# One new order for the last four images, u in two copies, and the up convolution in eight matrices from image 6 on

## The reference, cut to what matters

```
x = x + conv(group_norm(x))        # per image: repeat 2x, 12x12 up filter, leaky relu, 12x12 down filter, every second pixel
t = x as 1024 tokens of 32 channels
t = t + attention(layer_norm(t))   # causal, one head, 1024 x 1024 scores per image
t = t + ffn(layer_norm(t))         # per image: 16 experts each take their 8 best tokens, pool them by the softmax
                                   # over tokens, run two layers (gelu), and add the result back to those tokens
```

## Time and profile before

| | |
|---|---|
| median of 3 runs | 364.86 us (364.76 to 365.97) |
| the profiled execution | 366.71 us, of which the span from first to last instruction is 364.8 us |
| PE busy | 323.3 us (89%), weight loads 249.3 us (68%) |
| DVE, ACT, POOL busy | 258.4 us (71%), 186.6 us (51%), 127.3 us (35%) |
| up convolutions (line 923 into psB) | 480 matmuls |
| granted PE clock, mean | 0.954 |

### The profile page before, as it was taken

One profiled execution on the slowest core, in us unless ns is written; L12 is line 12 of the kernel. 1 busy time (PEld: TensorE's weight loads), 2 busy tenths in 40 slices (PEclk: granted clock), 3 DMA queues, 4 the chain that ended last, 5 costly groups with the idle time before them and its releaser, 6 DMA issues.

```text
span 364.8 us, 8376 instructions
## 1 busy us (share of the span) xinstructions
PE 323.3 (89%) x3357; PEld 249.3 (68%) x3357; DVE 258.4 (71%) x523; ACT 186.6 (51%) x257; POOL 127.3 (35%) x94
## 2 busy tenths in 40 slices
PE   2279998799999999999898998989998686996995
PEld 1168886587778778786767786858685444754894
DVE  2679779957766877859784877566988888265622
ACT  1043355457547574747664647466755647441510
POOL 6134635232444338454311374532116400043000
PEclk9999999999999999999999999999999999896655
DMA  4920000011010010101010101010103100100123
GB/s 123 195 49 3 23 22 16 15 17 31 16 18 23 8 32 2 31 2 34 15 16 2 31 0 32 2 31 5 26 15 74 34 2 6 42 2 29 47 68 88
DMA packets 35906, 11.16 MB, mean 31 GB/s; under 512 B 24431, under 2 KB 35741, under 8 KB 35869
## 3 DMA queue, kind: packets, MB, share of 16 engines
q1 hardware_dynamic: 33152, 9.98, 11.4%
q10 hardware_dynamic: 2717, 0.66, 1.3%
HBM read 5.72 MB, written 4.21 MB: 27 GB/s over the span
## 4 chain that ended last, share of the span: by engine, by line
PE 75%; DVE 10%; DMA 6%; issue 3%; ACT 3%; POOL 1%; SPq 1%; ACTq 1%; DVEq 0%; POOLq 0%
PE psB L923 14%; PE psA L923 13%; PE psB L1056 10%; PE psB L1036 8%; PE psA L1021 7%; PE psA L1114 5%; PE psA L1092 3%; PE psB L1073 2%; DVE negmax L784 2%; PE psA L1063 2%; PE psB L1039 2%; PE psA L911 2%; PE psA L1014 2%; PE psA L1024 2%; PE psB L1001 1%
## 5 line engine op out<-in xcount | busy, mean ns | idle before, releaser
L784 DVE TENSOR_REDUCE negmax<-psA 128x1 f32<-128x512 f32 (+7 forms) x128 | 90.7, 751 | 35.7 <-PE psA L1024 34.9
L596 ACT ACTIVATE Pp<-psB 128x1024 f32<-128x1024 f32 (+1 forms) x80 | 73.6, 938 | 34.9 <-PE psB L1039 30.8
L923 PE MATMUL psB<-xin,UU 128*128 128x224 f16 (+1 forms) x480 | 56.2, 276 | 0.2 <-issue 0.2
L923 PE MATMUL psA<-y,DD 128*128 128x224 f16 (+1 forms) x480 | 55.1, 273 | 0.0
L1021 PE MATMUL psA<-zK,yQ 128*128 128x512 f16 (+1 forms) x192 | 46.9, 326 | 7.1 <-DVE negmax L784 2.2
L923 PEld LDWEIGHTS psB<-xin,UU 128*128 128x128 f16 x480 | 46.9, 99 | 7.9 <-DVE xin L725 0.5
L1036 PE MATMUL psB<-yQ,zK 128*128 128x512 f16 (+1 forms) x192 | 47.2, 330 | 5.1 <-DMA yQ<-rows 2.8
L923 PEld LDWEIGHTS psA<-y,DD 128*128 128x128 f16 x480 | 46.8, 98 | 5.5
L486 POOL TENSOR_TENSOR zrstd<-zrstd,power 128x8 f32<-128x8 f32 x16 | 27.2, 1700 | 53.8 <-DVE zrstd L762 53.8
L566 ACT ACTIVATE y<-psB 128x1024 f16<-128x1024 f32 x16 | 16.4, 1023 | 44.5 <-PE psB L923 44.5
L508 POOL TENSOR_TENSOR y<-y 128x1024 f16<-128x1024 f32 x16 | 34.1, 2132 | 9.6 <-ACT y L569 9.6
(11 more groups left out here) (162 smaller groups left out, 499.4 us busy)
## 6 DMA issues: line engine op xcount, KB each, us to landing
x_all<-in_x_dram SPq DMA_DIRECT2D x4, 512.0 KB, 4.3
normalised_tokens<-z SPq DMA_DIRECT2D x16, 128.0 KB, 1.8
zV<-normalised_tokens SPq DMA_DIRECT2D x64, 32.0 KB, 2.2
out_dram<-x_all SPq DMA_DIRECT2D x8, 256.0 KB, 2.3
yQ<-rows SPq DMA_DIRECT2D x32, 2.0 KB
Pp<-filter_tables ACTq DMA_DIRECT2D x4, 121.9 KB, 4.2
w_halves<-y SPq DMA_DIRECT2D x12, 32.0 KB, 1.8
cst<-shape_constants SPq DMA_DIRECT2D x1, 326.5 KB, 4.3
```

The lines of the kernel that those rows point to most:

```text
L596: nc.scalar.activation(Pp[:, n % 2, UOFF[e[2]]:UOFF[e[2]] + N], slot(e)[:, 0:N], ACT.Exp).then_inc(b_drained, 1)
L784: ins = nc.vector.tensor_reduce(negmax[:, n % 2, m - 1:m], s[:, at:at + P * m], X, ALU.max, negate=True)
L923: ins = nc.tensor.matmul(within(out_cols, -shift), m, within(v, shift), start=i == 0, stop=i == len(matrices) - 1)
```

## The change

From image 6 on (`PLAIN_UP`), blocks t = 1 and 2 take one matrix for both neighbours: the taps of k = -1 for row blocks 2 and 3 are copied by two DMAs into the empty rows of the matrix of k = +1 (`filter_wrap`), and ScalarE makes moved copies of the image for it, partitions 0 to 63 moved one way, 64 to 127 the other (`mixed`, two activations an image, on a tile that POOL has set to zero). That makes 24 matmuls, all but six with 256 columns. Images 0 to 5 keep 30, but the three matmuls of k = +1 at t = 1 and 2 use only partitions 0 to 63, because the other rows of that matrix now hold something else. `wT` of groups 0 to 2 goes from ring B to ring A, its copy from ACT to DVE. u has two copies, by group; att has storage of its own, and the wait for the logits goes from `proj` to `uT`. The steps end at t = 11, and one new list holds everything from the last score of image 13 on. The core of the diff:

```diff
+LAST_STEP = 12
...
+PLAIN_UP = 6
...
+def mixture(ahead):
+
+    return lambda t: ("mixed", t + ahead) if PLAIN_UP <= t + ahead < B else None
...
-        once(-8, "xT", 3), batch(0, "prob", 0), group(6, "logit_max"), batch(2, "yQ"), batch(-1, "pv"),
+        once(-8, "xT", 3), batch(0, "prob", 0), mixture(5), group(6, "logit_max"), batch(2, "yQ"), batch(-1, "pv"),
...
-LAST = [("prob", B - 1, 0), ("pv", B - 2), ("prob", B - 1, 1), ("wT", G - 2), ("prob", B - 1, 2), ("mean", G - 1, 0), ("pool", G - 2),
-        ("prob", B - 1, 3), ("prob", B - 1, 4), ("square", G - 1, 0), ("proj", G - 1, 1), ("mean", G - 1, 1), ("dev", G - 1, 0),
-        ("pv", B - 1), ("hidden", 0), ("square", G - 1, 1), ("proj", G - 1, 2), ("mean", G - 1, 2), ("square", G - 1, 2), ("dev", G - 1, 1),
-        ("scale", G - 1, 0), ("experts", 0), ("dev", G - 1, 2), ("scale", G - 1, 1), ("turned", 0), ("scale", G - 1, 2), ("scatter", 1, 0),
-        ("uT", G - 1), ("logit_max", G - 1), ("logits", G - 1), ("select", G - 1), ("scatter", 1, 1), ("logit_exp", G - 1),
-        ("route", G - 1), ("scatter", 2, 0), ("scatter", 2, 1), ("wT", G - 1), ("pool", G - 1), ("scatter", 0, 0), ("hidden", 1), ("scatter", 0, 1), ("experts", 1),
-        ("turned", 1), ("scatter", G - 1, 0), ("scatter", G - 1, 1)]
+LAST = [("score", 13, 2), ("z_rstd", 15), ("prob", 12, 0), ("yQ", 14), ("dev", 2, 0), ("pv", 11), ("prob", 12, 1), ("score", 13, 0), ("prob", 12, 2),
+        ("proj", 2, 1), ("split_z", 15), ("score", 14, 4), ("shift", 13), ("prob", 12, 3), ("score", 14, 1), ("zK", 15), ("prob", 12, 4), ("score", 14, 3),
+        ("score", 14, 2), ("prob", 13, 0), ("yQ", 15), ("pv", 12), ("prob", 13, 1), ("score", 14, 0), ("mean", 2, 1), ("prob", 13, 2), ("score", 15, 4),
+        ("shift", 14), ("prob", 13, 3), ("score", 15, 1), ("prob", 13, 4), ("score", 15, 3), ("dev", 2, 1),
+        ("score", 15, 2), ("prob", 14, 0), ("pv", 13), ("score", 15, 0), ("prob", 14, 1), ("w1", 0), ("shift", 15), ("prob", 14, 2), ("w1", 1), ("uT", 2),
+        ("prob", 14, 3), ("proj", 3, 0), ("logits", 2), ("prob", 14, 4), ("mean", 3, 0), ("square", 3, 0),
+        ("prob", 15, 0), ("logit_max", 2), ("pv", 14), ("prob", 15, 1), ("proj", 3, 1), ("select", 2), ("logit_exp", 2), ("prob", 15, 2), ("mean", 3, 1),
+        ("route", 2), ("prob", 15, 3), ("dev", 3, 0), ("prob", 15, 4), ("wT", 2), ("square", 3, 1), ("pool", 2),
+        ("pv", 15), ("proj", 3, 2), ("dev", 3, 1), ("mean", 3, 2), ("hidden", 0), ("square", 3, 2),
+        ("scale", 3, 0), ("experts", 0), ("dev", 3, 2), ("scale", 3, 1), ("turned", 0), ("scale", 3, 2), ("scatter", 1, 0),
+        ("uT", 3), ("logit_max", 3), ("logits", 3), ("select", 3), ("scatter", 1, 1), ("logit_exp", 3),
+        ("route", 3), ("scatter", 2, 0), ("scatter", 2, 1), ("wT", 3), ("pool", 3), ("scatter", 0, 0), ("hidden", 1), ("scatter", 0, 1), ("experts", 1),
+        ("turned", 1), ("scatter", 3, 0), ("scatter", 3, 1)]
...
-    for t in range(-9, B - 1):
+    for t in range(-9, LAST_STEP):
...
-    return events + LAST
+    return [e for e in events if e not in LAST] + LAST
...
-ON_A = ("xT", "small", "dnT", "gn_mean", "gn_var", "proj", "score", "uT", "shift", "down", "pool", "yQ",
+ON_A = ("xT", "small", "dnT", "gn_mean", "gn_var", "proj", "score", "uT", "shift", "down", "wT", "pool", "yQ",
         "experts", "turned", "scatter")
-ON_B = ("up", "prob", "logits", "pv", "tok", "zK", "hidden", "wT")
-A = {e: n for n, e in enumerate(e for e in EVENTS if e[0] in ON_A)}
-BU = {e: n for n, e in enumerate(e for e in EVENTS if e[0] in ON_B)}
+ON_B = ("up", "prob", "logits", "pv", "tok", "zK", "hidden")
+LAST_WT = ("wT", G - 1)
+A = {e: n for n, e in enumerate(e for e in EVENTS if e[0] in ON_A and e != LAST_WT)}
+BU = {e: n for n, e in enumerate(e for e in EVENTS if e[0] in ON_B or e == LAST_WT)}
...
+        mixed = sb("mixed", [P, 2, 2, H, JW], F16)
...
-        att = uT
+        att = sb("att", [P, S])
...
-        u = sb("u", [P, KT, P])
+        u = sb("u", [P, 2, KT, P])
...
-        def part_of_u(first, last):
-            return u[:, :, C * first:C * last].rearrange("p k (b c) -> p b k c", b=last - first)
+        def part_of_u(n, first, last):
+            return u[:, n % 2, :, C * first:C * last].rearrange("p k (b c) -> p b k c", b=last - first)
...
+        def filter_wrap(r):
+
+            q, n = slice(C * r, C * r + C), r - 1
+            return (UU[q, :, SPAN - n:SPAN, :, :].rearrange("p i m q t -> p i (m q t)"),
+                    U_parts[q, :, 0:n, :, :].rearrange("p i m q t -> p i (m q t)"))
+
+        def mixture_halves(n):
+
+            at = BC * (n % GB)
+            v = xin[:, n // GB % 2, :].bitcast(F16).rearrange("p (i n) -> p i n", i=2)[:, :, at:at + BC].rearrange("p i (h j) -> p i h j", j=JW)
+            return [(mixed[rows, n % 2, :, :, to:to + JW - 1], v[rows, :, :, 1 - to:JW - to])
+                    for rows, to in ((slice(0, 2 * C), 0), (slice(2 * C, P), 1))]
...
+                    if g == 0:
+                        for r in (R - 2, R - 1):
+                            place_to, place_from = filter_wrap(r)
+                            sp.dma_start(place_to, place_from).then_inc(UU_wrapped, 16)
...
+                if name == "dnT":
+                    nc.gpsimd.memset(mixed[:, :, :, :, :], 0.0).then_inc(mixed_zero, 1)
...
-                    if g >= 1:
-                        pool.wait_ge(a_filled, A["pool", g - 1] + 1)
-                    nc.gpsimd.tensor_tensor(part_of_u(first, last), by_image(t2_all[:, g, :], first, last), per_token(nmean[:, e[2], :], last - first),
+                    if g >= 2:
+                        pool.wait_ge(a_filled, A["pool", g - 2] + 1)
+                    nc.gpsimd.tensor_tensor(part_of_u(g, first, last), by_image(t2_all[:, g, :], first, last), per_token(nmean[:, e[2], :], last - first),
...
+                if name == "mixed":
+                    if n < PLAIN_UP + 2:
+                        act.wait_ge(mixed_zero, 1)
+                    else:
+                        act.wait_ge(b_filled, BU["up", n - 2] + 1)
+                    act.wait_ge(xin_ready, 2 * (n // GB) + min(n % GB, 1) + 1)
+                    for to, v in mixture_halves(n):
+                        nc.scalar.activation(to, v, ACT.Copy).then_inc(mixed_ready, 1)
...
+                        act.wait_ge(UU_wrapped, 16 * 2)
...
                 elif name == "proj":
-                    if n >= 1:
-                        dve.wait_ge(b_filled, BU["logits", n - 1] + 1)
...
                 elif name == "uT":
+                    if n >= 1:
+                        dve.wait_ge(b_filled, BU["logits", n - 1] + 1)
...
+                elif name == "wT" and n < G - 1:
+                    if n >= 1:
+                        dve.wait_ge(a_filled, A["pool", n - 1] + 1)
+                    nc.vector.tensor_copy(wT[:, :, :].rearrange("p k n -> p (k n)"), s[:, 0:KT * GE]).then_inc(a_drained, 1)
...
+                    if n >= PLAIN_UP:
+                        pe.wait_ge(UU_wrapped, 16 * 2)
+                        pe.wait_ge(mixed_ready, 2 * (n - PLAIN_UP) + 2)
+                    of = slice(BC * (n % GB), BC * (n % GB) + BC)
+                    parts = [v[:, of] for v in img[n // GB % 2]]
+                    both = [mixed[:, n % 2, j, :, :].rearrange("p h j -> p (h j)") for j in range(2)]
                     for t in range(R):
+                        if 1 <= t <= 2 and n >= PLAIN_UP:
+                            outer = [(UU[:, i, R - t + NS - 1, :, :], both[j], 0) for i, j in ((0, 0), (0, 1), (1, 0))]
+                        else:
+                            outer = [(UU[0:rows, i, R * k - t + NS - 1, :, :], parts[j][0:rows], k)
+                                     for k, rows in ((-1, P), (1, 2 * C if 1 <= t <= 2 else P)) if 0 <= R * k - t + NS - 1 < SPAN
+                                     for i, j in ((0, 0), (0, 1), (1, 0))]
                         ins = convolve(s[:, BC * t:BC * t + BC],
-                                       [(UU[:, i, R * k - t + NS - 1, :, :], parts[j], k) for k in (-1, 0, 1) if 0 <= R * k - t + NS - 1 < SPAN
-                                        for i, j in ((0, 0), (0, 1), (1, 0))])
+                                       [(UU[:, i, NS - 1 - t, :, :], parts[j], 0) for i, j in ((0, 0), (0, 1), (1, 0))] + outer)
...
                 elif name == "pool":
                     if n == G - 1:
                         pe.wait_ge(wT_copied, 1)
+                    else:
+                        pe.wait_ge(a_drained, A["wT", n] + 1)
                     for k in range(KT):
-                        if k == R or n < G - 1:
-                            pe.wait_ge(b_drained, BU["wT", n] + 1)
-                        ins = nc.tensor.matmul(s[:, 0:GE], u[:, k, :], wT[:, k, :], start=k == 0, stop=k == KT - 1)
+                        if k == R and n == G - 1:
+                            pe.wait_ge(b_drained, BU[LAST_WT] + 1)
```

(39 more changed lines are left out.)

4 lines of the change are left out of this document (1 added, 3 removed).

## The result

The changed kernel is slower: 369.78 us median of four runs (369.36 to 370.48) beside 365.42 of before on the same chip, a ratio of 1.0115 (95% interval 1.0091 to 1.0138). The forecast was 361.5, with 365.3 as its upper end. The profiled execution took 370.2 us, its span 368.2 (before 366.71 and 364.8). The profiled execution of before lies 1.3 us above its median, so the two traces differ by 3.4 us where the medians differ by 4.4.

The account below looks back on a forecast made before the run. PE bounds the convolution part; VectorE and its chains set the pace from 276 to 310 us, one latency chain from 320. Terms -6.6 +1.5 +1.7 -1.9 +1.7 -0.3 +0.5 = -3.4 us off the 364.86 median: 361.5, range 357.0 to 365.3.

Parts of the forecast that it names:

- 60 matmuls less: Up convolutions from image 6 on: six of 30 matmuls go in each of ten images, 6.6 us less.
- changes of row count: Images 0 to 5: 24 switches between 128 and 64 rows at 0.09 us, two thirds counted, 1.5 us more.
- moved copies: ScalarE's two activations an image, 1.1 us, mostly hidden; late up for image 8 and late yQ add 1.7 us.
- wT on ring A: Steps 7 to 10: three bank conflicts go (2.8 us), one comes (about 0.9 us); together 1.9 us less.
- prob 12,0 to proj 3,2 (list and clock): Last part's new order: pv 15 starts 1.7 us later, plus 0.5 us for the clock.
- proj 3,2 to the end (u twice): Two copies of u take away GpSimd's 26 us wait for pool 2; only 0.3 us comes out of it.
- Rival 3: Images 0 to 5: all 24 row switches cost a drain of 0.27 us, 6.5 us, giving 366.5 us; 9%.
- The last part: From prob 12 on: late dev 2,1 delays group 2's root and routing chain, so pv 15 starts 1.7 us later.
- The clock: PE idles some 4 us ahead of wT 2; lower clock adds 0.5 us, between 0 and 1.7.
- Rival 4: Last part slips 3 us further by handovers and clock at 0.50 through pool 2 and pv 15: 364.5 us; 10%.
- Rival 1: New list pays: routing chain meets no VectorE waits or ScalarE queue, PE's gaps close, 4.9 us off, 356.6 us; 18%.

Follow-up runs that it names:

- run 2: Changed kernel with every up convolution at 30 full-height matmuls, no moved copies or wrapped taps; new list, u twice, wT on ring A stay: 370.34 us, ratio 1.0128.
- run 1: Changed kernel with the old order of the last part; u twice, wT on ring A and the new up convolution stay: 362.32 us, ratio 0.9905.
- run 7: Changed kernel with the old list and the wrapped taps in a filter tile of their own: 360.28 us, ratio 0.9842.
- run 11: As run 7, with ScalarE's moved copies one image ahead and at another place in its order: 359.17 us, ratio 0.982.
- run 12: As run 11, with the eight-matrix up convolution from image 2 on and wrapped taps fetched ahead of the first images: 359.13 us, ratio 0.982.
- run 3: Changed kernel with the wrapped taps in a filter tile of their own, so images 0 to 5 keep 128 rows: 366.29 us, ratio 1.0008.
- run 9: Changed kernel with mean 2,1 alone moved to behind prob 12,4, dev 2,1 left at its late place: ratio 1.0016.
- run 6: Changed kernel with nine idle matmuls ahead of wT 2 and three ahead of pool 2: 366.89 us, ratio 1.0026.
- run 10: Changed kernel with mean 2,1 and dev 2,1 moved earlier and idle matmuls ahead of wT 2 and pool 2: 362.65 us, ratio 0.9902.

## Why the prediction was wrong

By its own terms, forecast against measured (in us; the measured ones from the starts of events):

| term | forecast | measured |
|---|---|---|
| 60 matmuls less | -6.6 | -6.6 (ten times 0.66) |
| changes of row count | +1.5 | +2.5 (six times 0.42) |
| moved copies | +1.7 | +1.95 (0.97 + 2 x 0.41 + 0.16) |
| wT on ring A | -1.9 | -1.7 (run 2: -0.87 - 1.05 - 1.05 + 1.28) |
| what is left over up to prob 12,0 | 0 | +0.2 |
| prob 12,0 to proj 3,2 (list and clock) | +2.2 | +7.6 |
| proj 3,2 to the end (u twice) | -0.3 | -0.55 |
| sum | -3.4 | +3.4 (of the two traces; the medians +4.4) |

**Fewer matmuls, the ring, the moved copies:** right, within 0.3 us each. The pair of copies took 1.18 us, forecast 1.1. That 256 columns cost no more than 224 could not show, since they give one mean for 30 matmuls; the 0.66 us for six matmuls less bears it out. **u twice:** the last term came out near its number, but not from u twice alone. Runs 1, 7, 11 and 12, with u twice and the old list, take 40.2 to 40.8 us from proj 3,2 to the end, before 40.3, the changed kernel 39.75; so the 0.5 us need the new list.

**Half-height matmuls:** the price of a change was right (0.105 us; the row said 0.09 to 0.10), the share was not. I let gaps of PE take a third of it. The gaps of this stretch did not shrink (3.46 and 3.54 us), and run 3 got it back. Rival 3 was also priced too high: a start at the end of the matmul ahead, 0.27 us after its start in place of 0.11, adds 0.16 us and not 0.27, so 24 full waits are 3.9 us and not 6.5. The 0.105 us that came are two thirds of such a wait: the next matmul starts 0.205 us after the one ahead, 0.07 before its end, and that end is modelled. The rule of TensorEngine Tiling (Trainium skill, Tiling Modes), that a change of tiling mode drains TensorE, agrees with the runs in that a change costs something; a wait for the whole matmul they do not show.

**The last part is the step that failed.** It said that group 2's routing chain sets pv 15, and that its late root is what makes it late: 1.7 us. The order of the chain from uT 2 on was right, and even the root came within 1 us of the forecast (295.87, that is 299.5 on the old scale, forecast 298.5). This was in part luck: with mean 2,1 at its earlier place the same dev 2,1 puts the root at 292.98 (run 9). But nothing waited for the root: u was ready 1.6 us before PE came to uT 2. What was late was PE itself. I had followed the moved dev 2,1; of the moved mean 2,1 the forecast counts only the good (split_z 15 no longer waits behind it), and puts at nothing that its square stands on ScalarE ahead of three exponentials; the forecast names ScalarE's queue only for the exponential of the routing. That wait, its gap on PE and the clock behind it cost 3.8 us (run 9).

**The clock** was the second half of it. I took 0.5 us for a gap of 4 us ahead of wT 2. The gaps came at 2.08 and 0.88 us, and runs 6 and 10 put the price at 2.9 and 3.1: pool 2 1.65 us longer, pv 15 1.2. Rival 4 had named both (handovers and a clock at 0.50 through pool 2 and pv 15) with 10%, but with 3 us where 5.4 came. Rival 1 (the new list pays) looked true for a while: 4.4 us of gain between prob 12,0 and score 15,1, about 2 of them uT 2 and its wait put off, all of it lost behind it.

What stays open: what decides whether a gap is followed by half clock (the 2.2 us ahead of pv 14 were in before and in run 7, not in runs 1, 11 and 12), and why the new list, with both costs removed (run 10), still takes 1.8 us more from prob 12,0 to proj 3,2 than the old one in run 1 (51.38 and 49.57 us).
